# Layer norms behind layers 2 and 3 in two parts, and the node cell's biases inside the state's product, in a four-layer graph network on one core

## The reference

```python
x = _layernorm(x + relu(D * (A @ (x @ W)) * D + b))              # layer 1, A = adj + I
x = _layernorm(x + relu(softmax(where(adj > 0, leaky(f1 + f2.T), -9e15)) @ (x @ W)))   # layer 2
x = _layernorm(x + concat([(adj > 0) @ x, (adj < 0) @ x]) @ Wn + bn * dg
                 + (adj @ x) @ We + be * dg)                     # layer 3, dg = diag(adj)
# layer 4, An = adj without its diagonal
edge = gru_cell(An @ x, x, edge_Wih, edge_Whh, edge_bih, edge_bhh)
s = mean over 3 heads of (softmax(where(An > 0, e_plus, where(An < 0, e_minus, -9e15))) * An) @ (x @ W[k])
node = gru_cell(s, x, node_Wih, node_Whh, node_bih, node_bhh)
x = _layernorm(x + dg * edge + dg * node)

def gru_cell(x, h, Wih, Whh, bih, bhh):
    r = sigmoid(ir + hr); z = sigmoid(iz + hz); n = tanh(inn + r * hn)   # thirds of x @ Wih.T + bih and h @ Whh.T + bhh
    return (1 - z) * n + z * h
```

## Time and profile before

| | |
|---|---|
| median of 3 runs | 1465.62 us (1462.94 to 1467.64) |
| the profiled execution | 1466.58 us, its span 1465.0 us |
| TensorE busy | 1349.4 us, 92% of the span |
| VectorE, ScalarE, GpSimd busy | 906.4, 538.4, 194.7 us |
| TensorE's mean granted clock | 0.964 of full speed |

### The profile page before, as it was taken

One profiled execution on the slowest core, in us unless ns is written; L12 is line 12 of the kernel. 1 busy time (PEld: TensorE's weight loads), 2 busy tenths in 40 slices (PEclk: granted clock), 3 DMA queues, 4 the chain that ended last, 5 costly groups with the idle time before them and its releaser, 6 DMA issues.

```text
span 1465.0 us, 11467 instructions
## 1 busy us (share of the span) xinstructions
PE 1349.4 (92%) x4222; PEld 679.3 (46%) x4222; DVE 906.4 (62%) x1178; ACT 538.4 (37%) x459; POOL 194.7 (13%) x211
## 2 busy tenths in 40 slices
PE   3887887899979999998999999999999999999994
PEld 1333334344444444454655454644445444544541
DVE  4778777888864000102116363699978987898566
ACT  4343434867730000000111001455564556455333
POOL 0000002000020000001000000134521254122111
PEclk9999997999989999999889999999999999999997
DMA  9999992000027666657447339698876987688201
GB/s 380 428 421 427 418 380 85 0 0 0 0 102 195 193 194 194 187 148 257 134 157 233 110 108 328 223 361 325 307 283 239 334 311 281 247 329 308 95 0 49
DMA packets 78003, 321.29 MB, mean 219 GB/s; under 512 B 8684, under 2 KB 20587, under 8 KB 61035
## 3 DMA queue, kind: packets, MB, share of 16 engines
q1 hardware_dynamic: 77931, 320.40, 60.9%
HBM read 316.94 MB, written 3.43 MB: 219 GB/s over the span
## 4 chain that ended last, share of the span: by engine, by line
PE 83%; DMA 9%; DVE 4%; ACT 1%; issue 1%; SPq 0%; POOL 0%; ACTq 0%; DVEq 0%; POOLq 0%
PE ps L1282 29%; PE ps L1130 10%; PE ps L1095 10%; PE ps L1035 9%; DMA ring<-in_adjR 9%; PE ps L960 6%; PE ps L1089 5%; PE ps L1192 2%; PE ps L1302 1%; PE ps L1264 1%; PE ps L1111 1%; PE ps L1303 1%; PE ps L1072 1%; PE ps L1112 1%; PE ps L1151 1%; PE ps L1139 1%
## 5 line engine op out<-in xcount | busy, mean ns | idle before, releaser
L1282 PE MATMUL ps<-arena,x 128*128 128x512 f32 (+1 forms) x1092 | 438.9, 562 | 2.9 <-ACT shared L865 1.6
L1282 PEld LDWEIGHTS ps<-arena,x 128*128 128x128 f32 x1092 | 206.1, 190 | 231.4 <-issue 225.2
L858 ACT ACTIVATE arena<-arena,bench 128x3328 f32<-128x3328 bf16 x78 | 239.8, 3075 | 193.4 <-PE ps L1282 181.1
L960 PE MATMUL ps<-ring,bench 128*128 128x512 f32 (+1 forms) x364 | 168.2, 606 | 52.2 <-DMA ring<-in_adjR 50.1
L1916 DVE TENSOR_TENSOR arena<-arena,ring 128x3328 f32<-128x3328 f32 x51 | 184.9, 3625 | 26.5 <-ACT arena L858 25.9
L1095 PE MATMUL ps<-ring,x 128*128 128x512 f32 (+1 forms) x364 | 176.6, 567 | 0.0
L1130 PE MATMUL ps<-ring,x 128*128 128x512 f32 (+1 forms) x364 | 155.1, 582 | 3.7 <-DVE x L1448 3.7
L960 PEld LDWEIGHTS ps<-ring,bench 128*128 128x128 f32 x364 | 69.8, 203 | 129.5 <-issue 92.9
L1637 DVE SCALAR_TENSOR_TENSOR bench<-b,cols,ps 128x128 f32<-128x128 f32 x26 | 7.3, 343 | 189.0 <-PE ps L1072 189.0
L640 POOL TENSOR_TENSOR ring<-ring,nid 128x128 f32<-128x128 f32 x51 | 88.9, 1742 | 204.0 <-DMA ring<-in_adjR 204.0
L1130 PEld LDWEIGHTS ps<-ring,x 128*128 128x128 f32 x364 | 71.0, 197 | 77.4 <-issue 68.6
(11 more groups left out here) (288 smaller groups left out, 1430.1 us busy)
## 6 DMA issues: line engine op xcount, KB each, us to landing
ring<-in_adjR SPq DMA_DIRECT2D x77, 1664.0 KB, 8.8
ring<-in_adjB SPq DMA_DIRECT2D x312, 256.0 KB, 3.0
arena<-in_adjR SPq DMA_DIRECT2D x27, 1664.0 KB, 8.5
shared<-in_adj SPq DMA_DIRECT2D x7, 1664.0 KB, 13.4
es<-in_adj SPq DMA_DIRECT2D x7, 1664.0 KB, 13.4
xT<-in_adj SPq DMA_DIRECT2D x6, 1664.0 KB, 13.5
y<-in_adj SPq DMA_DIRECT2D x6, 1664.0 KB, 13.4
ring<-in_adjB SPq DMA_DIRECT2D x52, 128.0 KB, 2.2
```

The lines of the kernel that those rows point to most:

```text
L858: A_(E[n % 3], below[n % 3], ACT.Exp, bias=tt_[:, t * HEADS + k:t * HEADS + k + 1], scale=-WIN).then_inc(e_exp, 1)
L960: op = mm(ps[:, b, 0:w], lhsT=scaled[:, t % 4], rhs=turned_tile[t % 2][:, o_:o_ + w], start=(t == 0), stop=(t == TILES - 1))
L1282: last = mm(ps[:, b, 0:w], lhsT=x[:, t], rhs=E[n % 3][:, o_:o_ + w], start=(t == 0), stop=(t == TILES - 1))
```

## The change

Norm behind layer 2. `norm` falls into `variances` (statistics to mean and variance), `inverse_roots` and `norm_tile`. Tiles 0 to 11 (`PART1`) are normed inside the loop over pairs, from pair 8 on, tiles 12 to 25 behind it. ScalarE loads the square root's table ahead of layer 2's last steps. The Z1 products use other banks, so that banks 0 and 2, in which layer 3 begins, are free early.

Norm behind layer 3. Tiles 0 to 23 (`PART2`) are normed during the last block, each when that block's product has read it, tiles 24 and 25 behind it.

Head products. They move from ahead of layer 3 to behind its ninth tile, with one more: the last row of the node cell's state weights, spread over all rows. `late_steps` moves into layer 3's variant.

Node cell. The features of a normed x add up to zero, so the last one can be left out of a product if its row of the weights is subtracted from all others. In its place a one is put (`state_ones`, seven passes of ScalarE over `xT` during the second head), and that row of the weights holds the biases. The bias product and `split_bias` go.

```diff
+        PART1, PART2 = 12, 24
+        ONES_AT = [10 + 2 * b for b in range(NB)]
...
-            return ps[:, (7, 0, 1, 2, 3, 4, 5)[k % NB], :].rearrange("p (a n) -> p a n", a=2)
+            return ps[:, Z1_BANKS[k], :].rearrange("p (a n) -> p a n", a=2)
+        Z1_BANKS = (7, 0, 1, 2, 3, 4, 5, 7, 1, 3, 4, 5, 6)
...
+                A_(zf[:, 0:1], ones[:, 0:1], ACT.Sqrt)
                 act.wait_ge(small, XSB_READY)
...
                     relu_pair(k)
+                    if k == PART1 // 2 + 1:
+                        roots(1, 0, PART1)
...
+                roots(2, PART1, TILES)
...
+                if b == NB - 1:
+                    roots(3, 0, PART2)
                 act.wait_ge(ring_free, CHUNKS + R2 + (b + 1) * TILES)
...
-            roots(2)
+            roots(4, PART2, TILES)
...
+                A_(xT[:, o_:o_ + w], xT[:, o_:o_ + w], ACT.Identity, scale=others[:], bias=lone[:]).then_inc(ones_in, 1)
...
                         weights(k, t)
+                        if k == 1 and t in ONES_AT:
+                            state_ones(ONES_AT.index(t))
...
-                    last = max(k // 2, k - 1 if k < NB else 0)
+                    last = max(k // 2, k - 1 if k < NB else 0, NB - 1 if k == GROUPS - 1 else 0)
...
-                    if k >= NB:
-                        pe.wait_ge(z_out, 2 + GROUPS + k - NB + 1)
+                    if Z1_BEFORE[k] is not None:
+                        pe.wait_ge(z_out, 2 + GROUPS + Z1_BEFORE[k] + 1)
...
+            def heads_vectors():
+                pe.wait_ge(late_in, W_LATE)
+                pe.wait_ge(z_out, 2 + 2 * GROUPS)
+                for k in range(HEADS):
+                    mm(ps[:, 6, 2 * k:2 * k + 2], lhsT=gWT[:, k], rhs=ga[:, k], start=True, stop=True)
+                mm(ps[:, 6, P:P + G3], lhsT=lone[:].to_broadcast([P, P]), rhs=gru[:, 3], start=True, stop=True).then_inc(late_prod, 1)
...
                            stop=final).then_inc(ring_free, 1)
+                        if n == 8 and not negative:
+                            heads_vectors()
...
-                            mm(gt[:, 0:4 * F], lhsT=ones16, rhs=bias_parts, start=True, stop=False)
-                            mm(gt[:, F:4 * F], lhsT=ut, rhs=gru[:, 2], start=False, stop=False)
-                            last = mm(gt[:, 0:G3], lhsT=ht, rhs=gru[:, 3], start=False, stop=True)
+                            mm(gt[:, 0:4 * F], lhsT=ht, rhs=state_weights, start=True, stop=False)
+                            last = mm(gt[:, F:4 * F], lhsT=ut, rhs=gru[:, 2], start=False, stop=True)
...
-                split_bias()
+                step(v.scalar_tensor_tensor(state_weights[:, 0:G3], state_weights[:, 0:G3], lone[:], gru[:, 3], ALU.mult, ALU.add))
+                step(v.tensor_scalar(state_weights[:, G3:], state_weights[:, G3:], lone[:], None, ALU.mult))
+                step(v.tensor_scalar(others[:], lone[:], -1.0, 1.0, ALU.mult, ALU.add))
...
                     if k >= 2:
                         finish1(k - 2)
+                    if k == PART1 // 2 + 1:
+                        variances(GROUPS + PART1 // 2, 0, PART1)
+                    if k == PART1 // 2 + 2:
+                        inverse_roots(1, 0, PART1)
+                    if k > PART1 // 2 + 1:
+                        norm_pair(k - PART1 // 2 - 2)
...
             either(ve, layer3, 0)
+            variances(2 * GROUPS + PART2 // 2, 0, PART2)
+            inverse_roots(3, 0, PART2)
+            for t in range(PART2):
+
+                ve.wait_ge(ring_free, CHUNKS + R2 + (NB - 1) * TILES + t + 1)
+                norm_tile(t)
             finish3(NB - 1)
-            norm(2)
+            variances(3 * GROUPS, PART2, TILES)
+            inverse_roots(4, PART2, TILES)
+            for t in range(PART2, TILES):
+                norm_tile(t)
```

More of the change, by code:

```diff
@@ L1456, in split_x, with inverse_roots, norm_tile, norm_pair @@
+            def inverse_roots(n, lo, hi):
+                ve.wait_ge(root, n + 1)
+                step(v.reciprocal(rstd[:, lo:hi], std[:, lo:hi]))
+            def norm_tile(t):
+                v.tensor_scalar(tile(x, t), tile(y, t), column(mean, t), column(rstd, t), ALU.subtract,
+                                ALU.mult).then_inc(x_done, 1)
+            def norm_pair(c):
+                norm_tile(2 * c)
+                norm_tile(2 * c + 1)
+                split_x(c)
             def split_x(c):
@@ L1507, in _ @@
             statistics0(GROUPS - 1)
-            norm(0)
+            variances(GROUPS, 0, TILES)
+            inverse_roots(0, 0, TILES)
+            for t in range(TILES):
+                norm_tile(t)
+                column_scores(t)
             def faint_row():
@@ L1993, in node @@
                         node_stats(g - 2)
-                norm(3)
+                variances(4 * GROUPS, 0, TILES)
+                inverse_roots(5, 0, TILES)
+                step(v.scalar_tensor_tensor(diff, mean, -1.0, rstd, ALU.mult, ALU.mult))
+                check(steps[0], OUT_READY)
+                for t in range(OUT_VE):
+                    norm_tile(t)
             def heads_and_node(general):
```

110 lines of the change are left out of this document (55 added, 55 removed).

## The result

| | before | after |
|---|---|---|
| median of the runs shown | 1466.53 us (4 runs, 1462.94 to 1467.64) | 1451.18 us (4 runs, 1450.19 to 1454.53) |
| profiled execution | 1466.58 us | 1450.85 us |
| its span | 1465.0 us | 1449.1 us |

The ratio is 0.991, with a 95% interval of 0.9891 to 0.9929. The forecast was 1453.1 us in a range of 1448 to 1460. Later the changed kernel was run again, on one chip with the kernel before, and gave 1450.86 against 1465.89 us, a ratio of 0.9892 (0.9876 to 0.9909).

A forecast was written before the change was run, and what follows sets the result against it. TensorE was taken to carry 83% of the chain of waits; 0.65 + 5.5 + 6.4 = 12.55 us off the profiled 1466.58 gave 1454.0, less 0.96 to the median 1453.1 us, range 1448 to 1460.

The forecast's parts named there:

- Seam 2 to 3: Between layers 2 and 3: earlier start 1.65, low clock 0.5, head products -1.5; 0.65 us gained (-2.6 to +2.1).
- The step with the branch: Ahead of layer 3: TensorE's branch lands 0.76 us later, at 432.3; layer 3 starts at 433.0, gaining 1.65 us.
- the second flag: Ahead of layer 3: the flag's load and second branch behind TensorE's first branch, taken as 0.7 us (0 to 3.1).
- Seam 3 to 4: Between layers 3 and 4: 3.75 us idle goes, clock stays up for 1.8 more; 5.5 us gained (3.7 to 5.6).
- The cover of 4.4 us: Ahead of layer 4: tile 0 ready 4.4 us before TensorE asks, gone only if VectorE's branch costs over 10.8 us.
- Node cell: Node cell at the end: a group takes 3.34 instead of 3.83 us, 6.4 us gained (7.5 without loss behind the turns).
- ScalarE's passes: Second head: seven passes over xT at 0.69 us each stay hidden; 4.8 us if the cover is gone.
- (a): Rival: node cell gains nothing, the loss belonging to the place or VectorE's chain taking over; 1459.5 us, chance 0.12.
- theory S: Node cell: about 0.1 us lost twice at each bf16/float32 change; 1454.9 us for run 5, 1461.0 for run 6.
- (b): Rival: the seam between layers 3 and 4 gains nothing, VectorE's branch or the norms being late; 1458.6 us, chance 0.07.
- (c): Rival: ScalarE's seven passes in the second head come through to the path; 1457.9 us, chance 0.03.
- (d): Rival: layer 3's block 0, fed pair by pair, stays at 1.2 GHz throughout; slower, 1484 us, chance 0.04.

The follow-up runs named there:

- run 1: Changed kernel with TensorE's jump over layer 2's general variant moved to the start of layer 2: 1449.94 us, ratio 0.9896.
- run 6: Kernel before, with the bias products of a node-cell group's two tiles side by side ahead of the float32 products: 1462.40 us, ratio 0.9978.
- run 5: Kernel before without the node cell's bias product, the state's product written to the other's 384 columns (result not the reference's): 1454.55 us, ratio 0.993.
- run 3: Changed kernel with layer 2's norm in one piece behind the loop over pairs again: 1456.70 us, ratio 0.9944.
- run 4: Kernel before with the node cell's part of the change alone, both norms in one piece: 1457.26 us, ratio 0.9953.
- run 2: Changed kernel with layer 3's norm in one piece behind finish3(6) again: 1454.70 to 1457.72 us in three executions, 7559.85 in a fourth, ratio 0.9943.
- run 7: Changed kernel as it is, run and profiled once more beside the kernel before: 1450.86 us, ratio 0.9892.

## Why the prediction held, and where it did not

The time was forecast at 1453.1 us and came out at 1451.2. The forecast sum was 12.55 us; the ledger without the luck of layer 4 is 1.2 + 5.7 + 7.6 = 14.5.

- **Seam 2 to 3, forecast 0.65, measured 1.18 (again 1.14).** The step with the branch was right as a mechanism: run 1 shows that the jump held TensorE. That the start moved by 1.64 us against a forecast of 1.65 is luck, since two sizes were off and cancel. Z1 ends 1.28 us later behind its start (427.59 - 419.85 = 7.74 against 6.46) and not 0.76, because two pairs of products and not one stand behind the wait for relu pair 6 (the row at 426.46). And the idle stretch behind it grew by 0.19 us (6.12 against 5.93) where 0.7 was put for the second flag; this stretch varied by more than that between executions (5.44 to 6.62), so no run gives the second flag's price. That the idle time would be labelled "issue" was wrong for this profile, it bore VectorE's name; whoever had gone by the label would have put work into x16. The low clock gave 0.85 instead of 0.5, the head products took 1.31 instead of 1.5, both within their bounds.
- **Seam 3 to 4, forecast 5.5, measured 5.71 (again 5.72).** Idle time and clock both as reckoned. VectorE's branch was priced at 6.40 us, the price of its only visible one, and took 2.00. The cover of 4.4 us was thus wider than stated. VectorE's other branch, ahead of the late steps, shrank to 3.37 us in the changed kernel. The price of one jump, read in one place, is not that of the next.
- **Node cell, forecast 6.4, measured 7.63.** This is the term that was mis-sized most. The 0.09 us behind the turns was read in the rows and then left standing, for want of a reason why it should go; it went, since it belongs to the bias product that followed (run 6). The text had named 7.5 for that case. The row that could have decided it stands right behind the first of the earlier trace rows: two passes of 128 columns take 917.94 - 917.72 = 0.22 us in the edge cell.

```profile
917.94 0.81 PE L1111 MATMUL ps<-gru,xT 128*128 128x384 f32 x2
```

- **ScalarE's passes, nothing forecast, nothing measured.** They took 0.80 us each rather than the 0.69 of the row that was taken for them; they are hidden all the same.
- **What the sum left out:** 2 us in the profiled execution, 3.33 gained behind the small products of layer 4 less 1.27 at the stop for a transfer. The distance between profile and median, 0.96 us, which was subtracted at the end, is no property of the kernel either: with a fourth run the median before is 1466.53, 0.05 under the profile. Against that median the sum would have forecast 1454.0.
- **The rivals.** (a) fell in runs 5 and 6: the loss goes with the bias product, not with its place. That it comes from unlike types, as the prediction and theory S had it, is not borne out by layer 3 (run 6); what they forecast was right all the same, since only the loss itself enters the sum. The Trainium skill ("TensorE: Matmul & The Clock Gate", Back-to-back issue gap) prices a single product by its columns, N/2.4 + 2.5 ns. The products with x16 in layer 3 agree (0.43 us for two of 512). Float32 beside float32 follows its columns too, but at twice that price (1.29 us for 1536 column-passes in run 6, 0.84 ns each). And the rule leaves out the 0.29 us a tile that the bias product loses besides. (b) fell with the 2.00 us. (c) with the head's unchanged idle time. (d) with a clock that rose in the second tile.

**Left open.** The norm of layer 2 in two parts is worth 0.98 us by the trace at its seam, yet the kernel without it (run 3) was 5.5 us slower in all four executions, spread over only 1.4 us, while eight executions of the changed kernel spread over 6.1. Against the repeated profile of the changed kernel, the slower of its two, the profile of run 3 loses one step of 1.68 us at the second row of small products and 0.54 at the stop for a transfer; with the 0.94 by which it was behind already, this makes about the 3.1 us between the two at the end, counted behind Z1's start. The three other executions have no trace. Whether the moment at which layer 4 begins decides how long the clock stays low, so that a kernel is lucky or unlucky as a whole, was not tested. If so, a part of what is called luck here goes with the change.

## What to carry to other kernels

When an engine idles ahead of a stage and the code holds a variant that is not run, look for the jump over it, whatever engine the profile names, and put the jump where the engine waits anyway. A product of few rows between products of 128 rows cost more than its columns here: fold it into a neighbour that grows by as many, or put such products side by side. Test a cause against rows elsewhere in the same trace before giving it a name: layer 3 had spoken against "another type" from the start. An idle stretch that cannot be closed is room for small products that stand on the path elsewhere.

## What the runs showed of the hardware

- **A taken jump over an unused variant cost TensorE up to 6.6 us.** The idle times that it ended were 5.93 (before), 5.44 (run 4), 6.12 (changed kernel), 6.24 (again) and 6.62 us (run 2); the last three include the load of the second flag. That it was the jump is shown for the changed kernel, where run 1 took it away; the others have it in the same place. On VectorE 6.40, 3.37 and 2.00 us were seen behind its jumps. The Trainium skill ("Runtime: NRT & Kernel Launch", Instruction fetch mechanics) says that a taken branch to a target outside the pages held forces a fetch; run 1 agrees in that the idle time went with the jump, but no run shows the fetch itself.
- **A product of three rows between products of 128 rows cost about 0.1 us at each of three places**: entering it (0.32 against 0.22), leaving the last such product (0.53 for two of 0.216 each), and at the first product behind it (0.75 against 0.65). It did so in bf16 and in float32 alike, while products of 128 rows in bf16, or float16 with fp8, between float32 ones lost 0.05 us or nothing (run 6).
- **Some of VectorE's operations grow where GpSimd's additions run beside them;** that these are the cause is read from the times alone. In the first pair of norms behind the reciprocals the two norms took 1.09 us instead of 0.58, and from the second pair on the cast of 256 columns took 0.70 instead of 0.29 (timeline of VectorE, changed kernel):

```profile
431.88 0.70 DVE L1494 CAST shared<-x 128x256 f16<-128x256 f32 x1
...
441.73 0.29 DVE L1494 CAST shared<-x 128x256 f16<-128x256 f32 x1
```

- **While the rows of 6- and 3-column products ran, without a gap, the granted clock fell from 1.00 to 0.50** (2.4 to 1.2 GHz), and the tiles behind them pay: five tiles took 5.96 to 7.58 us for the same work. How much they pay differs between executions of one program, in steps of 1.6 to 1.7 us (run 7).
